# A gated attention and expert kernel: the denominators of the twelve long units summed by TensorE in PSUM instead of by VectorE

## The reference

```python
x = x + tanh(g_xattn[0]) * wkv(time_decay, time_first, layernorm(x), ctx)
x = x + tanh(g_ffn[0]) * moe(layernorm(x), Wg, bg, W1, W2)

# wkv, for each batch and channel, k = layernorm(x), v = ctx, w = -exp(time_decay), u = time_first
y_t = (sum_{s<t} exp(k_s + (t-1-s) * w) * v_s + exp(u + k_t) * v_t) / (the same with v = 1)

# moe: logits = x @ Wg + bg, softmax over the best 2 of 4 experts; expert i takes the 512 tokens of
# the largest probability p and adds p * (gelu(tok @ W1[i]) @ W2[i]) to their rows
```

## Time and profile before

| | us |
|---|---|
| median of 3 runs (478.63 to 479.13) | 478.77 |
| the profiled execution | 477.77 |
| its span, first to last instruction | 476.0 |
| PE busy | 414.5 (87%) |
| VectorE busy | 292.1 (61%) |
| ScalarE busy | 313.1 (66%) |
| GpSimd busy | 108.0 (23%) |

### The profile page before, as it was taken

One profiled execution on the slowest core, in us unless ns is written; L12 is line 12 of the kernel. 1 busy time (PEld: TensorE's weight loads), 2 busy tenths in 40 slices (PEclk: granted clock), 3 DMA queues, 4 the chain that ended last, 5 costly groups with the idle time before them and its releaser, 6 DMA issues.

```text
span 476.0 us, 7146 instructions
## 1 busy us (share of the span) xinstructions
PE 414.5 (87%) x2039; PEld 201.4 (42%) x2039; DVE 292.1 (61%) x596; ACT 313.1 (66%) x487; POOL 108.0 (23%) x126
## 2 busy tenths in 40 slices
PE   2586877712899999999999999999999999999991
PEld 2343343401554444454444444444444444444440
DVE  7999999988499976564674155457514635560000
ACT  6798888998669773926778780577879147760000
POOL 0787746701300002521001311100041110001111
PEclk9999998955699999999999999999999999999997
DMA  7994120499400828438001925600092310001211
GB/s 265 341 351 180 44 90 1 161 343 360 129 2 0 349 91 291 109 74 326 0 0 61 372 52 196 204 0 1 11 374 79 42 24 0 0 0 9 36 22 22
DMA packets 23126, 59.64 MB, mean 125 GB/s; under 512 B 1280, under 2 KB 1408, under 8 KB 21056
## 3 DMA queue, kind: packets, MB, share of 16 engines
q1 hardware_dynamic: 19008, 50.17, 28.5%
q0 software_dynamic: 3664, 8.65, 9.0%
q10 hardware_dynamic: 432, 0.54, 0.3%
HBM read 46.78 MB, written 12.58 MB: 125 GB/s over the span
## 4 chain that ended last, share of the span: by engine, by line
PE 74%; DVE 15%; issue 3%; ACT 2%; POOL 2%; DMA 1%; ACTq 0%; DVEq 0%; POOLq 0%
PE ps L818 35%; PE ps L803 26%; PE ps L781 7%; DVE arena L1280 6%; PE ps L744 2%; DVE arena L1299 2%; DVE arena L1310 2%; PE ps L714 1%; DVE arena L1536 1%; DMA arena<-xn_table,idx 1%; PE ps L610 1%; ACT early L883 1%; POOL arena L1139 1%; PE ps L736 1%; DVE arena L1658 0%
## 5 line engine op out<-in xcount | busy, mean ns | idle before, releaser
L818 PE MATMUL ps<-arena 128*128 128x512 f16 x768 | 167.7, 379 | 0.0
L803 PE MATMUL ps<-arena,early 128*128 128x512 f16 x576 | 124.8, 379 | 0.0
L818 PEld LDWEIGHTS ps<-arena 128*128 128x128 f16 x768 | 74.6, 98 | 88.1
L803 PEld LDWEIGHTS ps<-arena,early 128*128 x576 | 56.3, 98 | 68.0
L1046 ACT ACTIVATE arena<-ps,up 128x512 f32<-128x512 f32 x64 | 43.8, 684 | 58.6 <-PE ps L803 40.0
L1709 DVE SCALAR_TENSOR_TENSOR arena<-arena,h_down 128x512 f32 x48 | 36.1, 751 | 58.9 <-ACT arena L1049 58.9
L1218 POOL DMA_INDIRECT result<-arena,idx x16 | 27.6, 1724 | 191.0 <-DVE arena L1737 137.8
L1049 ACT ACTIVATE arena<-arena,h_down 128x512 f32 x64 | 46.2, 721 | 8.7 <-ACT arena L1046 0.2
L1689 DVE SCALAR_TENSOR_TENSOR early<-w_raw,down,early 128x2048 f16<-128x2048 f32 x16 | 37.1, 2346 | 18.9 <-ACT early L1007 18.8
L1737 DVE TENSOR_SCALAR arena<-ps,yscale 128x512 f32<-128x512 f32 x16 | 12.0, 748 | 59.1 <-PE ps L818 49.1
L1052 ACT ACTIVATE arena<-rows,down x64 | 45.2, 706 | 0.0
(11 more groups left out here) (226 smaller groups left out, 461.2 us busy)
## 6 DMA issues: line engine op xcount, KB each, us to landing
w_raw<-in_L_ffn_W SPq DMA_DIRECT2D x4, 4096.0 KB, 13.9
rows<-in_L_ffn_W SPq DMA_DIRECT2D x3, 4096.0 KB, 17.6
rows<-in_L_ffn_W SPq DMA_DIRECT2D x4, 1024.0 KB, 9.2
result<-rows SPq DMA_DIRECT2D x3, 1024.0 KB, 6.8
early<-in_ctx SPq DMA_DIRECT2D x2, 1024.0 KB, 6.3
rows<-in_x SPq DMA_DIRECT2D x2, 1024.0 KB, 11.0
xn_table<-arena SPq DMA_DIRECT2D x4, 512.0 KB, 5.2
xn_table<-arena SPq DMA_DIRECT2D x2, 1024.0 KB, 4.8
```

The costliest lines, as they stand in the source:

```text
L803: last = nc.tensor.matmul(ps[:, PH[q], :], w[:, k, at], t[:, k, :], start=n == 0, stop=n == 3 * CT - 1)
L818: last = nc.tensor.matmul(ps[:, PY[s % 2], :], h[:, t, s * P:(s + 1) * P], w[:, t, :], start=t == 0 and n == 0, stop=t == HT - 1 and n == 2)
```

## The change

In a long unit the denominator is no longer an addition of VectorE. ScalarE scales the identity by c once for each of the four channel blocks (`first_diag`, 128x128 fp32 each, at the start). PE then multiplies it with the 512 columns of state and adds the result onto the transposed keys in their PSUM bank (`add_first`), and the logarithm of ScalarE reads them from PSUM. The keys of unit u + 2 go into the same bank, so they can be transposed only after the logarithm of unit u: `kv` is cut into `keys` and `products`, and in steps of long units the keys come after products, x and router. In step 2 x is transposed ahead of the products (`LATE_M`). Short units keep the addition on VectorE. The semaphore s_kv becomes two, s_keys and s_kv, and each place that waited for it waits for both; three semaphores elsewhere are dropped and their waits put on others. den shrinks by as many columns as first_diag takes, so nothing else in the arena moves.

```diff
@@ -104,6 +104,7 @@
 NORMS2 = {8: (0,), 9: (1,), 14: (2,), 15: (3,), 16: (4,), 17: (5,), 18: (6,), 19: (7,)}
 SUMS = (11, 14, 15)
 EDGE2 = (0, 2, 6, 10, 13, 16)
+LATE_M = CT - 2
 COPY_AT = CT * (NG - 1)
 
 
@@ -202,7 +203,8 @@
         at = [0]
         mv = part(arena, at, (RING, D))
         decay = part(arena, at, (CT, 2 * UN))
-        den = part(arena, at, (2, UN))
+        den = part(arena, at, (2, SEQ))
+        first_diag = part(arena, at, (CT, P))
         num = part(arena, at, (2, UN))
         rden = part(arena, at, (2, UN))
         y_a = part(arena, at, (2, UN))
@@ -476,6 +478,14 @@
         def length(u):
 
             return GROUPS[u // CT] * SEQ
+
+        def long(u):
+
+            return GROUPS[u // CT] > 1
+
+        def shorts(u):
+
+            return sum(not long(i) for i in range(u + 1))
 
         def starts(ap, u):
 
@@ -563,13 +573,36 @@
 
             def kv(u):
 
+                keys(u)
+                products(u)
+
+            def keys(u):
+
                 g, ct = u // CT, u % CT
                 if u >= 2:
-                    pe.wait_ge(s_den if GROUPS[g] > 1 else s_num, u - 1)
+                    pe.wait_ge(s_num, u - 1)
+                    if long(u - 2):
+                        pe.wait_ge(s_ln, u - 1)
                 for i, t in enumerate(tiles_of(g)):
                     if ct == 0:
                         pe.wait_ge(s_ek, t + 1)
-                    nc.tensor.transpose(pair(u, length(u) + i * P, length(u) + (i + 1) * P), ek[:, t % RING, ct * P:(ct + 1) * P], ident)
+                    last = nc.tensor.matmul(pair(u, length(u) + i * P, length(u) + (i + 1) * P), ek[:, t % RING, ct * P:(ct + 1) * P], ident,
+                                     start=i == 0 or not long(u), stop=True, is_transpose=True,
+                                            skip_group_check=True)
+                last.then_inc(s_keys, 1)
+
+            def add_first(u):
+
+                size = length(u)
+                if u == CT:
+                    pe.wait_ge(s_diag, CT)
+                pe.wait_ge(s_fix, u + 1)
+                nc.tensor.matmul(pair(u, size, 2 * size), first_diag[:, u % CT, :], state[:, u % 2, size:2 * size],
+                                 start=False, stop=True, skip_group_check=True).then_inc(s_denp, 1)
+
+            def products(u):
+
+                g, ct = u // CT, u % CT
                 if u >= 2:
                     pe.wait_ge(s_num, u - 1)
                 for i, t in enumerate(tiles_of(g)):
@@ -626,13 +659,22 @@
                 last = nc.tensor.matmul(ps[:, PL, 0:E], ones32[:, :], wg_raw[:, k, :], start=k == 0, stop=k == CT - 1)
             last.then_inc(setup_p, 1)
             for u in range(UNITS):
+                if long(u):
+                    add_first(u)
+                elif u + 2 < UNITS:
+                    keys(u + 2)
+                if u == LATE_M:
+                    xt(u)
                 if u + 2 < UNITS:
-                    kv(u + 2)
+                    products(u + 2)
                 if u == UNITS - 1:
                     residual_rows(TT - SPT - 1)
-                xt(u)
+                if u != LATE_M:
+                    xt(u)
                 if u > 0:
                     router(u - 1)
+                if long(u):
+                    keys(u + 2)
                 for t in rows_out(u):
                     if u < UNITS - 1:
                         residual_rows(t)
@@ -897,6 +940,9 @@
             act.wait_ge(setup_a, 5)
             for k in range(CT):
                 set_decay(k, 0)
+            act.wait_ge(s_id, 16)
+            for k in range(CT):
+                nc.scalar.activation(first_diag[:, k, :], ident, ACT.Copy, scale=chan[:, 3, k:k + 1]).then_inc(s_diag, 1)
             start(act, c_tokhi, c_w1hi, c_w2hi, c_gelu, c_hhi, c_w2sum, c_w1sum)
 
             def take_rows(t):
@@ -931,10 +977,15 @@
             def one_over_den(u):
 
                 cols = slice(0, length(u))
-                act.wait_ge(s_den, u + 1)
+                if long(u):
+                    act.wait_ge(s_denp, u - shorts(u) + 1)
+                    there = pair(u, length(u), 2 * length(u))
+                else:
+                    act.wait_ge(s_den, shorts(u))
+                    there = den[:, u % 2, cols]
                 if u >= 2:
                     act.wait_ge(s_y, u - 1)
-                nc.scalar.activation(rden[:, u % 2, cols], den[:, u % 2, cols], ACT.Ln,
+                nc.scalar.activation(rden[:, u % 2, cols], there, ACT.Ln,
                                      scale=chan[:, 5, u % CT:u % CT + 1]).then_inc(s_ln, 1)
                 act.wait_ge(s_ln, u + 1)
                 nc.scalar.activation(rden[:, u % 2, cols], rden[:, u % 2, cols], ACT.Exp, scale=-1.0).then_inc(s_r, 1)
@@ -1273,10 +1325,13 @@
 
                 size = 2 * length(u)
                 dve.wait_ge(s_kv, u + 1)
+                dve.wait_ge(s_keys, u + 1)
                 if u < 2 * CT:
                     dve.wait_ge(s_decay, u + 1)
                 if u >= 2:
                     dve.wait_ge(s_num, u - 1)
+                    if long(u - 2):
+                        dve.wait_ge(s_denp, u - 2 - shorts(u - 2) + 1)
                 nc.vector.tensor_tensor_scan(state[:, u % 2, 1:size + 1], decay[:, u % CT, 0:size], pair(u, 0, size),
                                              0.0, ALU.mult, ALU.add).then_inc(s_scan, 1)
 
@@ -1290,10 +1345,11 @@
 
                 n, size, c = u % 2, length(u), chan[:, 3, u % CT:u % CT + 1]
                 dve.wait_ge(s_fix, u + 1)
-                if u >= 2:
-                    dve.wait_ge(s_ln, u - 1)
-                nc.vector.scalar_tensor_tensor(den[:, n, 0:size], state[:, n, size:2 * size], c, pair(u, size, 2 * size),
-                                               ALU.mult, ALU.add).then_inc(s_den, 1)
+                if not long(u):
+                    if u >= 2:
+                        dve.wait_ge(s_ln, u - 1)
+                    nc.vector.scalar_tensor_tensor(den[:, n, 0:size], state[:, n, size:2 * size], c, pair(u, size, 2 * size),
+                                                   ALU.mult, ALU.add).then_inc(s_den, 1)
                 if u >= 2:
                     dve.wait_ge(s_y, u - 1)
                 nc.vector.scalar_tensor_tensor(num[:, n, 0:size], state[:, n, 0:size], c, pair(u, 0, size),
```

More of the change, by code:

```diff
@@ L351, in program @@
         s_m = sem("m_rows_ready")
-        s_kv = sem("m_and_ek_transposed")
+        s_keys = sem("ek_transposed")
+        s_kv = sem("m_transposed")
         s_xt = sem("x_transposed")
@@ L356, in program @@
         s_den = sem("den_ready")
+        s_denp = sem("den_in_psum")
+        s_diag = sem("first_diagonals_set")
         s_num = sem("num_ready")
@@ L881, in exp_rows @@
                 if t >= RING:
+                    act.wait_ge(s_keys, CT * (group_of(t - RING) + 1))
                     act.wait_ge(s_kv, CT * (group_of(t - RING) + 1))
@@ L1070, in _ @@
                            prob[:, :, :].rearrange("p t e -> p (t e)").unsqueeze(2).to_broadcast([P, TT * E, LANES])).then_inc(g_wide, 1)
+            act.wait_ge(s_keys, UNITS)
             act.wait_ge(s_kv, UNITS)
@@ L1230, in _ @@
                 pool.wait_ge(s_x1st[g], 16)
-            nc.gpsimd.memset(none[:, :], 0).then_inc(c_zero, 1)
-            pool.wait_ge(c_zero, 1)
+            nc.gpsimd.memset(none[:, :], 0).then_inc(s_mhalf, 1)
+            pool.wait_ge(s_mhalf, 3)
             nc.gpsimd.indirect_dma_start(tok[:, ST - 1, :], None, xn2_table, bass.IndirectOffsetOnAxis(ap=none[:, 0:1], axis=0),
@@ L1452, in _ @@
             step(nc.vector.tensor_reduce(psum_r[:, :], pex[:, :, :], AX.X, ALU.add))
-            nc.vector.reciprocal(psum_r[:, :], psum_r[:, :]).then_inc(b_rsum, 1)
-            dve.wait_ge(b_rsum, 1)
+            step(nc.vector.reciprocal(psum_r[:, :], psum_r[:, :]))
             for n in range(2):
@@ L1482, in scales_of @@
                 dve.wait_ge(c_wpow2, START + count)
-                nc.vector.tensor_copy(up[:, m:m + 1], wpow[:, m:m + 1]).then_inc(c_wpow3, 1)
+                nc.vector.tensor_copy(up[:, m:m + 1], wpow[:, m:m + 1])
                 nc.vector.reciprocal(down[:, m:m + 1], wpow[:, m:m + 1]).then_inc(c_down, 1)
```

3 lines of the change are left out of this document (removed).

## The result

The changed kernel took **474.3 us** (median of 6 runs, 473.86 to 476.84) against 478.7 for the kernel before (6 runs, 477.75 to 479.13): a ratio of 0.9921, interval 0.9897 to 0.9945. The profiled execution took 475.27 us around a span of 473.5.

What follows compares the result with a forecast made beforehand. PE was to replace VectorE as bound at 4.51 us a full unit, with unit 15's matmul at 76.2. Then -1.7 at the end and +0.4 in short units gave -1.3: 478.8 - 1.3 = 477.5 us, range 475.9 to 480.6.

Steps and rivals of the forecast that it cites:

- four groups of transposes at 0.66 and the router at 0.88, net: PE's work in one long unit before the change: 3.52 of 4.50 us, leaving 0.98 slack.
- PE takes over as the bound, and these seven steps gain nothing: Steps 5 and 8 to 13: PE needs 3.52 + 0.99 = 4.51 us, against 4.50 before.
- The new matmul: One fp32 matmul of 128 columns by 512 on PE per long unit: 0.99 us, bounds 0.88 to 1.32.
- the first rival: Weight loads of the new matmul hidden on PE: 0.88 us each, total 476.6 us; chance 0.18.
- The doubts about a load of 0.11 or 0.22: Exposed weight loads on PE: both at 0.11, 1.10 a matmul (chance 0.20); both at 0.22, 1.32 (chance 0.14).
- VectorE still the bound: Rival for the long units: PE faster than its rows, -7.9 us, total 470.9; chance 0.03.
- I allow 0.6 for PE's waits on rows from GpSimd: Allowance in PE's steps up to unit 15, putting unit 15's new matmul at 76.2 instead of 75.6.
- The start: Units 2 to 5: x of unit 2 earlier gains 0.3; slow clock loses 0.5; unit 5's new matmul at 32.5.
- The half clock at the first new matmul: Step 4: PE still at half clock until 28.9, costing +0.5 us; the step takes 4.6.
- The end: Behind unit 15: exposed chain, unit 17's scan at 80.7 instead of 82.36, -1.7; short units give back +0.4.
- one sequence whose parts I expect to shift as a whole: The chain from the end of the units to the kernel's end, expected to shift as a whole.
- scans 4.8 apart: Sign against the prediction in the attention units' scans: such spacing would mean the matmul is dearer.

Runs made afterwards that it cites:

- the kernel with three orders changed: The change with products last in steps 6, 10 and 14, GpSimd's second-norm roots a step later, and its quotient before the scales in step 11: 471.2 us.
- the second execution: The change once more, unaltered, for a second profile: 474.81 us, span 472.5.
- two changes of order: The change with products last in steps 6, 10 and 14 and GpSimd's first second-norm roots a step later: 471.89 us.

## Why the prediction was wrong

**The step that failed** is "four groups of transposes at 0.66 and the router at 0.88, net", and with it "PE takes over as the bound, and these seven steps gain nothing". Measured with PE's waits met, the four groups take 0.44, 0.53, 0.49 and 0.44, together 1.90 instead of 2.64. That is 0.74 of the error of 0.80; the matmul adds 0.13 (0.86 for 0.99), and the router takes 0.07 back (0.95 for 0.88).

The rows could have told it. In the earlier trace rows the denominator, numerator and residual start at 55.00, 55.66 and 56.32, 0.66 apart, and each releases a group on PE: the keys wait for the denominator's end, the products for the numerator's, x for the residual's. The 0.66 was **VectorE's spacing**, seen on PE. The weight-load rows of that unit of before would have named the waits:

```profile
55.80 0.42 PEld L572 LDWEIGHTS ps<-cst,early 128*128 128x128 f32 x4 [1.22 <-DVE arena L1295]
56.46 0.42 PEld L578 LDWEIGHTS ps<-cst,arena 128*128 128x128 f32 x4 [0.24 <-DVE arena L1299]
57.12 0.42 PEld L587 LDWEIGHTS ps<-cst,rows 128*128 128x128 f32 x4 [0.24 <-DVE arena L1310]
```

The loads of the products and of x each stood 0.24 us for a semaphore of VectorE, and those of the keys 1.22. The prediction read the matmuls' line, which shows no gap at the products and at x, and took a queue of short waits for work. The rows' group had no such wait, but for it I took the modelled duration, 0.66, instead of a start-to-start distance. That a group's own price is 0.44 is shown by the kernel with the keys twice.

**The new matmul.** 0.86 from start to start, more where the products behind it stood for the numerator (0.89 at 54.73); 0.99 was forecast, 0.88 was the lower end. No time for the loads is left in 0.86: they are hidden, as the first rival had it. The Trainium skill ("TensorE: Matmul & The Clock Gate", "Step-by-step: what each phase is for") says that loads are pulled ahead of matmuls in flight; the trace agrees, with the loads at 58.97 for a matmul at 59.08. The doubts about a load of 0.11 or 0.22 are settled by the kernel with two matmuls: 0.86 for each.

**VectorE still the bound**, with a chance of 0.03, was the right picture of the steady units: scans 3.84 apart wherever nothing is late. "PE would have to fit in 3.84, less than its old parts and any matmul of 512" is the sentence that the wrong price led to. Its total, 470.9, did not come, but the kernel with three orders changed came to 471.2.

**GpSimd.** "I allow 0.6 for PE's waits on rows from GpSimd": the five units lost 3.2, and most of it not on PE but on VectorE, as late quotients. The 0.94 of unit 12 is in part ScalarE's own list, as the last kernel showed: in the change run again the logarithm of unit 11 starts at 59.37, behind ScalarE's squares, 0.8 after the matmul that it needs, and GpSimd adds 0.56 (the exponential ends at 60.70, the quotient starts at 61.26). The prediction had looked at GpSimd's product rows for one unit only, at the end, and never at what stands ahead of its quotients. Of the gain of 7.9, 3.2 went there, and 1.04 of the 1.50 given back behind unit 15 too, for that much returned with the products last. At 4.50 us a unit all of this was covered (the quotient moved first on the kernel before: 1.0003). At 3.84 it is covered as well as long as the new matmul is missing; with it, it isn't. So the matmul costs little of PE's time and more by where it stands, ahead of the logarithm, exponential and quotient.

**The start.** x of unit 2 earlier: -0.3 forecast, 0.35 measured, on either kernel. The half clock at the first new matmul (+0.5) was not there: the matmul at 28.05 was followed by the products at 28.99, and the router at 26.86 already took 0.59, as the fast one in the earlier trace rows. The term falls: step 4 took 3.50 from matmul to matmul (28.05 to 31.55), where 4.6 was forecast. That PE was at 1.2 GHz until then is read from durations alone (1.02 for the router at 24.32, 0.59 at 26.86): the granted clock is 1.00 from 24 to 28 us, and also from 8 to 12 us before the change, where the prediction took the 0.23 of the earlier trace rows to be at half clock. So halving that 0.23 was an assumption; no run tests it.

**The end.** Matmul to logarithm 1.06 (forecast 0.99 + 0.06), from there to the quotient's end 2.70 (2.74), and 4.38 from the scan of unit 16 to 17 (4.4). In the short units 0.25 was given back (0.24 in the second execution; forecast 0.4). The first three held; the last was smaller than forecast. The new matmul of unit 15, forecast at 76.2, came at 76.01, but for a different reason: not by PE's work of 43.1 us but by waits. It starts 3.76 after its unit's scan, behind PE's wait of 1.46 for GpSimd at 73.65; with the products last in step 14 it starts 2.60 after it (69.77 to 72.37), and the way from scan 16 to 17 fell to 3.35.

**The sum.** In the first profile the last scan comes 1.64 earlier, and the residual of the last unit 1.55 (forecast 1.3 for both). That close hit is chance: an error of 0.80 in each full PE step, and of 1.1 in step 4, stood against too small an allowance for GpSimd and a stretch at half clock. From the new matmul of unit 5 to that of unit 15 the forecast had 43.7 us (43.1 and the 0.6); it was 44.46, of PE steps that needed far less and waits that filled them. In the execution without that stretch the last scan comes 2.98 earlier. Add the shorter gather, 0.50 to 0.71, which was "one sequence whose parts I expect to shift as a whole", and the spans are 2.5 and 3.5 shorter. The medians differ by 4.4 and 3.8. In the first pair the profiled execution of before lay 0.9 under its median, and that of the change, the one with the half clock, 1.0 over its own.

The signs set down beforehand did their work: "The prediction is wrong if the scans come 3.9 apart (PE has room)" is what the profile shows wherever nothing is late. Its other sign, scans 4.8 apart "(the matmul is dearer)", would have misled: the profile has three units of 4.78 to 5.24 beside the one with the half clock, and in them VectorE stood for a quotient.

## What to carry to other kernels

A queue's spacing is its price only where none of its instructions waits, and a wait of a quarter microsecond shows on the weight loads, not on the matmuls: before an engine is called full, look for the releaser in every row, and compare its spacing with that of the engine that feeds it. When the bound's unit gets shorter, walk through every helper engine's list once with the new unit, for what it has ahead of each thing that the bound waits for; here late rows and quotients of GpSimd took 3.2 us and more of 7.9, though only because the new matmul also made each logarithm later, and two changes of order brought 2.9 back. Moving an urgent instruction ahead is safe only if nobody has urgent work behind what it passed: the same edit was worth 0.16 us by the scans in step 11, and with step 8 it cost 1.4 us.

## What the runs showed of the hardware

- fp32 transposes of 128x128 in a row take 0.11 us each when the loads run ahead (the change: 0.44 for four; the keys twice: 0.44 more for four more). A group whose first load has to wait takes 0.59 to the next (before: 57.12 to 57.71).
- An fp32 matmul of 128 columns of weights by 512 takes 0.86 us at the full clock, less than the same with 4 columns (0.95), whose loads begin only with their own first pass (both at 57.71) while the wider ones begin 0.11 ahead; that this is the reason wasn't tested. Its modelled duration, 1.02 to 1.13 at the full clock, was 1.43, 1.69 and 1.92 in three profiles in which it met the half clock.
- The clock of the same kernel at the same place differed from one execution to the next: in the stretch from 38 to 42 us 0.71 for the change, 1.00 for the change run again. In the eight profiles with the m rows late in that step PE stood for them twice, 0.68 to 0.94 us each (in one of the eight once, 0.48), and three of the eight had the dip there (0.71, 0.57, 0.68); with the products moved behind, none of three had. What sets it off in some executions alone is open. By the scans from unit 7 to 9 it cost 1.6 us (10.05 against 8.41, the two profiles of the change).
- ScalarE's logarithm of 128x512 takes 0.66 to 0.69 us from PSUM (the change), 0.71 to 0.72 from SBUF (before).
